# The last scatter products of a routed feed-forward: rounded parts of all four tiles first, on a signal of ScalarE

## The reference

```python
shared = einsum(gelu(einsum(xf, sW1) + sb1), sW2) + sb2      # mean over two shared experts
topk_vals, topk_idx = top_k(xf @ rW + rb, 2)                 # 8 experts, two for each row
w = sum(softmax(topk_vals) * onehot(topk_idx))
y = einsum(gelu(einsum(xf, W1) + b1), W2) + b2               # hidden width 2048
out = x + shared + sum_e w[:, e] * y[e]                      # 512 rows of 512
```

## Time and profile before

| what | value |
|---|---|
| median of 3 runs | 1206.45 us (1204.71 to 1206.72) |
| the profiled execution, its own time | 1206.51 us |
| its span, first to last instruction | 1204.8 us |
| TensorE busy | 1198.4 us (99% of the span) |
| VectorE busy | 834.9 us (69%) |
| ScalarE busy | 686.2 us (57%) |
| GpSimd busy | 589.6 us (49%) |
| granted TensorE clock, mean | 0.999 of full speed |

### The profile page before, as it was taken

One profiled execution on the slowest core, in us unless ns is written; L12 is line 12 of the kernel. 1 busy time (PEld: TensorE's weight loads), 2 busy tenths in 40 slices (PEclk: granted clock), 3 DMA queues, 4 the chain that ended last, 5 costly groups with the idle time before them and its releaser, 6 DMA issues.

```text
span 1204.8 us, 33750 instructions
## 1 busy us (share of the span) xinstructions
PE 1198.4 (99%) x14478; PEld 1126.1 (93%) x14478; DVE 834.9 (69%) x1210; ACT 686.2 (57%) x1247; POOL 589.6 (49%) x371
## 2 busy tenths in 40 slices
PE   9999999999999999999999999999999999999998
PEld 8999999999999999999999999898989999999997
DVE  7777777786877886876876867765765555655456
ACT  5465666656756656556756568455444455544453
POOL 5767777776867776867767664000051010000043
PEclk9999999999999999999999999999999999999999
DMA  8331111221111122121122135855456699999991
GB/s 297 103 112 37 43 41 41 77 72 46 64 56 73 43 71 77 37 84 43 41 72 77 44 113 206 311 187 180 160 175 217 233 353 338 336 348 360 353 372 71
DMA packets 34985, 179.65 MB, mean 149 GB/s; under 512 B 6368, under 2 KB 9632, under 8 KB 15760
## 3 DMA queue, kind: packets, MB, share of 16 engines
q1 hardware_dynamic: 32416, 170.32, 38.5%
q0 software_dynamic: 2416, 7.12, 1.8%
HBM read 168.97 MB, written 8.46 MB: 147 GB/s over the span
## 4 chain that ended last, share of the span: by engine, by line
PE 97%; POOL 1%; DVE 1%; issue 0%; DMA 0%; ACT 0%; DVEq 0%; POOLq 0%
PE bank L996 20%; PE bank L999 19%; PE bank L1361 12%; PE sc L1378 9%; PE sc L1019 8%; PE sc L1219 7%; PE bank L1038 4%; PE sc L1239 4%; PE bank L1239 4%; PE bank L1107 1%; PE bank L968 1%; PE bank L1161 1%; PE bank L1064 1%; PE sc L1179 1%; POOL blk L731 1%; PE bank L914 1%
## 5 line engine op out<-in xcount | busy, mean ns | idle before, releaser
L777 POOL TENSOR_TENSOR xn<-xn,tt 128x1024 f32<-128x1024 f32 x96 | 230.1, 2397 | 141.3 <-DVE tt L1716 139.2
L1814 DVE TENSOR_TENSOR wsl<-ring,wsh 128x2048 fp32r<-128x2048 f32 x72 | 168.7, 2345 | 126.5 <-ACT wsh L1467 126.5
L999 PE MATMUL bank<-wvh,blk 128*128 128x256 f32 x1344 | 247.6, 286 | 0.0
L996 PE MATMUL bank<-blk,wkh 128*128 128x256 f32 x1344 | 245.9, 285 | 0.0
L1533 ACT ACTIVATE tt<-sc 128x512 f32<-128x512 f32 (+1 forms) x208 | 107.8, 603 | 207.7 <-PE sc L1019 204.8
L996 PEld LDWEIGHTS bank<-blk,wkh 128*128 128x128 f32 x1344 | 209.3, 192 | 4.2 <-issue 1.6
L999 PEld LDWEIGHTS bank<-wvh,blk 128*128 128x128 f32 x1344 | 209.6, 192 | 2.7 <-issue 0.2
L999 PE MATMUL bank<-wvl,blk 128*128 128x256 f32 x672 | 190.4, 283 | 0.0
L996 PE MATMUL bank<-blk,wkl 128*128 128x256 f32 x672 | 190.2, 283 | 0.0
L1467 ACT CAST wsh<-ring 128x2048 fp32r<-128x2048 f32 x72 | 137.4, 1910 | 75.2 <-PE sc L1239 27.8
L1361 PEld LDWEIGHTS bank<-xT,ring 128*128 128x128 f32 x1280 | 144.6, 192 | 0.9
(11 more groups left out here) (333 smaller groups left out, 2201.2 us busy)
## 6 DMA issues: line engine op xcount, KB each, us to landing
ring<-in_w SPq DMA_DIRECT2D x112, 1024.0 KB, 6.7
stg<-in_ctx SPq DMA_DIRECT2D x24, 1024.0 KB, 5.0
wqt<-in_wo SPq DMA_DIRECT2D x4, 1024.0 KB, 5.2
wqt<-in_aq SPq DMA_DIRECT2D x4, 1024.0 KB, 5.4
wqt<-in_ap_ SPq DMA_DIRECT2D x4, 1024.0 KB, 5.0
yrows<-K SPq DMA_DIRECT2D x1, 2048.0 KB, 12.3
bsum<-in_tails SPq DMA_DIRECT2D x4, 260.0 KB, 5.4
ktail<-bsum SPq DMA_DIRECT2D x1, 1040.0 KB, 4.9
```

The source lines that it names most:

```text
L777: e.tensor_tensor(dacc[0:kn, y, :], dacc[0:kn, y, :], tt[0:kn, w, :], ALU.add).then_inc(s["da_pool"], 1)
L996: m = e.matmul(dst[:, 256 * a:256 * a + 256], w[:, WPOS[j], c, r], x[:, c, :], start=(k_ == 0), stop=(k_ == 5))
L999: m = e.matmul(dst[:, 256 * a:256 * a + 256], x[:, c, r], w[:, WPOS[j], c, :], start=(k_ == 0), stop=(k_ == 5))
L1814: e.tensor_tensor(wsl[m % 3][:], ring[slot(unit_split(m))][:], wsh[m % 3][:].bitcast(F32), ALU.subtract).then_inc(s["wl_dve"], 1)
```

## The change

For the last block the eight scatter products change order: the four with yh, for tiles 0 to 3, come first, and then the four with yl. The first four no longer wait for VectorE's last signal but for a new one, last_act, which a drain of ScalarE raises behind its own `rest(NE)`, and for none_dve (VectorE zeroed yh, yl and GT in block 4, for the case in which no block is scattered). The four with yl wait for last_dve as before, and each raises end_pe. Since GT must be there too, TensorE now waits for gt_dve at the end of every block from 8 on, and not ahead of the scatter inside the next block. Order and signals of the scatter inside blocks stay.

```diff
-            def scattered(signal):
-
-                for t in range(4):
-                    for x_, y_ in enumerate((yh, yl)):
-                        m = e.matmul(bank[4 + t][:], GT[:, 0, P * t:P * t + P], y_, start=False, stop=True,
-                                     skip_group_check=True)
-                    if signal == "end_pe" or t == 3:
-                        m.then_inc(s[signal], 1)
+            def scattered(t, y_):
+
+                return e.matmul(bank[4 + t][:], GT[:, 0, P * t:P * t + P], y_, start=False, stop=True,
+                                skip_group_check=True)
...
                     if q == 1 and k > NDIR:
                         e.wait_ge(s["yl_dve"], k - NDIR)
-                        e.wait_ge(s["gt_dve"], k - NDIR)
-                        scattered("sc_pe")
+                        for t in range(4):
+                            for y_ in (yh, yl):
+                                m = scattered(t, y_)
+                        m.then_inc(s["sc_pe"], 1)
...
                     m.then_inc(s["rd_pe"], 1)
+                if k >= NDIR:
+                    e.wait_ge(s["gt_dve"], k - NDIR + 1)
...
             e.matmul(bank[7][:], ident[:], xres[:, 3, :], start=False, stop=True, skip_group_check=True)
+            e.wait_ge(s["none_dve"], 3)
+            e.wait_ge(s["last_act"], 1)
+            for t in range(4):
+                scattered(t, yh)
             e.wait_ge(s["last_dve"], 1)
-            scattered("end_pe")
+            for t in range(4):
+                scattered(t, yl).then_inc(s["end_pe"], 1)
...
             rest(NE)
+            e.drain().then_inc(s["last_act"], 1)
             e.wait_ge(s["end_pe"], 4)
             e.copy(xres[:, 3, :], bank[7][:]).then_inc(s["sum_act"], 1)
```

More of the change, by code:

```diff
@@ L399, in build @@
             "wkh_act wvh_act wsh_act th_act kt_act ch_act t_act ln_act ex_act rstd_act xth_act wqh_act q_act "
-            "exp_act woh_act xh_act gap_act wT_act ge_act wh_act rg_act yh_act sum_act "
+            "exp_act woh_act xh_act gap_act wT_act ge_act wh_act rg_act yh_act last_act sum_act "
             "eps_dve iota_dve ones_dve cs_dve un_dve wkl_dve wvl_dve tl_dve kt_dve bias_dve xr_dve f_dve "
```

## The result

The changed kernel takes 1207.83 us (median of 22 runs, 1206.19 to 1209.29), the kernel before 1205.55 us beside it (22 runs, 1204.19 to 1207.01): ratio 1.0018, 95% interval 1.0012 to 1.0024. By the ratio that is 2.2 us slower (the two medians are 2.28 us apart). The time lies inside the range of the prediction, but it moved clear of its noise, and the forecast was that it would not.

The account below looks back on a forecast made before the run. TensorE's stream bounds the kernel up to 1197 us, then a tail of some 8 us. From the profiled 1206.51 us: -0.05 - 0 + 0 = 1206.46, so 1206.4 for the median; range 1204.7 to 1208.0 us.

Parts of the forecast that it names:

- the signal of ScalarE: Behind the last yh: ScalarE's drain runs 1197.72 to 1197.94 us, so a scatter product may start at 1197.99.
- rival 2: At ScalarE's jump over five blocks: code must be fetched, signal and end 1.5 us later, 1207.9 us; chance 0.10.
- The 1.5 us: Rival 2's price for one fetch: the larger instruction packet in flight, 3.2% of 16 engines x 3 us.
- the upper end of the range: Top of the forecast range, set by rival 2 (1207.9 us): 1208.0 us.
- the price of the jump: At the last jump: L1392 starts 0.36 us behind the last product, 0.13 more than usual, and that stays.
- the order's arithmetic: Last scatter: 0.70 us earlier start is spent on tiles 1 to 3; tile 0 finishes 0.05 us earlier.
- The wait for gt_dve: At TensorE's branches: signals are there over 8 us before anything waits, cost nothing; bound 0.7 us together.
- tile 3's 0.79 us: Tail: tile 3 and ScalarE's copy finish 0.79 us earlier, at 1200.05, but give nothing at the end.
- the two reasons given: Against tile 3's gain showing: SyncE issues transfers in tile order, and DMA engines are full 1201.25 to 1203.75 us.
- A measurement tells about 0.2%: Whole kernel: a difference is told from none at about 0.2%, 2.4 us; chance of same 0.90.

Follow-up runs that it names:

- 48 dead instructions: Changed kernel with ScalarE's code for block 14 left out and 48 ACTIVATE that never run added in block 13; one run, tail 10.51 us.
- drain only: Kernel before plus ScalarE's drain behind the last block, whose signal nobody waits for; ratio 1.0005, tail 7.71 us.
- waits only: Kernel before with only the wait for gt_dve moved to the end of each block from 8 on; ratio 0.9997, tail 7.77 us.
- tile 3 second: Kernel before with the last products, sums and transfers in tile order 0, 3, 1, 2; ratio 1.0000, tail 7.84 us.
- order alone: Kernel before with the last eight products as four yh then four yl, behind the wait for last_dve; ratio 1.0008, tail 8.33 us.
- ScalarE short: Changed kernel with ScalarE's code for blocks 10 to 14, which don't run, left out; ratio to the kernel before 1.0009, tail 7.70 us.
- the changed kernel again: The changed kernel unaltered, measured and profiled a second time; ratio to the kernel before 1.0019, tail 9.92 us.
- the kernel before with both short: Kernel before with the code of blocks 10 to 14 left out for ScalarE and TensorE; ratio 1.0001, tail 7.60 us.
- the kernel with 240: Changed kernel with ScalarE's jump over block 10 alone and 240 ACTIVATE that never run added in its code; one run, tail 9.59 us.

## Why the prediction was wrong

By its own steps:

- **The step that failed is "the signal of ScalarE".** The prediction took VectorE's drain as the nearest row and put ScalarE's signal 0.8 us behind the start of yh. It came 2.70 us behind it, and 3.0 in the second profile. VectorE's exit from the same branches, with its drain 0.59 us behind the start of yl, was the argument against rival 2; it says nothing about ScalarE, whose code for a block is longer (31 records and 21). With ScalarE's jump made short, the drain was at 0.5 us, or with yh when there was none, and the jump's part of the tail was gone; with 48 dead instructions it was back at 2.8.
- **Rival 2 is what happened**, with a chance of 0.10 and 1.5 us for a fetch. Measured: 2.1 to 2.4 us more than a short jump, 1.86 and 2.25 us more in the tail. The median moved by 2.2. The 1.5 us were the q8 packet of the earlier trace rows, which goes with TensorE's jump; ScalarE's, 0.7% of 16 engines x 3 us, is 0.3 us. That rival 2's 1207.9 us is so close to the measured 1207.83 is luck: its price was 0.6 to 0.9 us too low, and its start, the median of three runs, 0.9 us above that of 22. From 1205.55 the same working gives 1207.0 for rival 2 and 1207.1 for the upper end of the range, and 1207.83 lies above both.
- Rival 2 rested on the Trainium skill, "Advanced Engine Details and Errata", section ISA Cache, which gives two lines of 16 KB for a sequencer's code, and that was the right lead. What the runs show agrees with code held in pieces: a step with the length of code, and none with the number of branches. That the wait is a fetch is argued from this step and from the packet that goes with the jump; no row names it. The 16 KB that the Trainium skill gives for a line are the size of the packet that goes with TensorE's jump here; ScalarE's is of 8 KB.
- **TensorE's jump was missed altogether.** The prediction read the gap ahead of L1392, 0.13 us, as the price of the jump. The rows of the branch say 3.5 us, hidden behind the products that are still queued; what shows is its end. When block 9 is held up just ahead of its last twelve products, the branch starts late, and L1392 with it, by 0.6 to 1.0 us behind yh. In the order of the kernel before, the wait for VectorE's drain covers that but for 0.07 to 0.25 us by which tile 0's closing product is later (drain only, waits only, tile 3 second); with four products put between L1392 and tile 0's closing one, it no longer does: tails of 8.2 to 8.5 us with ScalarE in time, 7.65 with both jumps gone. That is one profile for each kernel; the medians with short jumps, 1.0005 to 1.0009 and 0.9999, are not apart beyond their intervals.
- Of the rest, the order's arithmetic held: 0.7 us for tile 0's closing product in fifth place, measured 0.66 in the tail. With the signal in time its last product started 0.03 us later than before, and with both jumps gone 0.03 us earlier, where 0.09 earlier to 0.01 later was forecast.
- The wait for gt_dve costs nothing that can be told, as forecast (0.9997). Its margin was smaller than worked out: TensorE's branch is reached at 1193.5 us, ahead of its products, and not at 1197, so GT, done at 1189.0, was there 4.5 us before and not over 8.
- That tile 3's 0.79 us are hidden was right: with ScalarE's jump gone its copy was done 0.67 us ahead of the third sum, and the tail was as before. Of the two reasons given, the full DMA engines are enough by themselves; whether the order of the queue would hold it back too was hardly tested.
- "A measurement tells about 0.2%" was too modest for 22 runs against 22: the interval is 0.06% to each side, and 2.2 us stood clear of it.

Each of the two changed-kernel profiles carries the loss in the tail. What block 9 does ahead of it varies from profile to profile in all kernels: GpSimd's first four additions (of the stored rows to x) take 5.0 us in five profiles and 7.0 to 8.7 us in the other eleven, and VectorE's splits of weights in that stretch take between 2.3 and 3.4 us. The five had no stall of TensorE in block 9 (the kernel before, order alone, ScalarE short, the changed kernel again, the kernel before with both short), nine of the eleven had one of 0.5 to 1.3 us. The two others of the eleven had no such stall, and their L1392 was late all the same (0.56 and 0.95 us behind yh). What decides how long GpSimd's additions take was not tried.

## What to carry to other kernels

An engine's way out of code that is skipped was not free here (2.5 us on ScalarE, 3.6 on TensorE) and not the same on all engines: look at the sequencer's rows, the branch and the instruction behind it, on the engine that is to give the new signal. A delay on an engine that nobody waits for did not show in the list of waits; it showed when a signal was put behind it. And before a product is moved forward, ask which product closes the first tile, as the sums and the transfers hang on that one.

## What the runs showed of the hardware that was not expected

- ScalarE's first instruction behind a jump over five blocks of its code starts 2.6 to 2.9 us behind the start of yh, at which the branch is done; over one to four 0.5 us. Code that never runs decides it (48 instructions more: 2.8 us). VectorE's drain behind its jump over the same five blocks, in less code, starts 0.59 us behind yl in all profiles.
- TensorE's branch over the same five blocks takes 3.5 to 3.9 us, 0.18 us at the most when there is nothing to jump over. It is taken ahead of the products that are still queued, so that most of it is hidden. L1392 starts 0.23 us behind the last product of block 9 when there is nothing to jump over, 0.3 to 0.7 us in the four profiles with the jump and GpSimd's additions at 5.0 us, and 1.0 to 1.4 us in the ten others.
- In the kernel with 48 dead instructions TensorE stood still for 0.99 us, made L1392, stood still for 0.93 us, and 0.4 us later its clock was granted at half: mean 0.55 in the window of the eight scatter products, which were then 0.43 us apart and not 0.235. That is 1.2 in place of 2.4 GHz, and most of the 0.9 us by which its tail is longer than that of the kernel with 240. In the changed kernel, with 0.78 and 0.96 us of standing still, the window has 1.00, and so it has in the kernel with 240 (0.91 and 0.83 us) and in the changed kernel's second profile (0.32 and 1.75 us). It was seen in one run, and what decides it is open. The kernel with 48 first, then the changed kernel:

```profile
1199.10:1202.50 3.40, 3.40 (x8) 2.20 (x8) 1.12 (x2) 0.00 (x0) 0.00 (x0) 0.55 0.01 2
```

```profile
1200.20:1202.30 2.10, 2.10 (x8) 1.40 (x8) 0.59 (x1) 0.00 (x0) 0.00 (x0) 1.00 0.01 4
```
